# A decoder layer on one core: values kept at 64 features a head, and heads joined by the output matrix afterwards

## What is computed

```python
xn = layernorm(x) * gamma
q = (xn @ w_q).reshape(b, n, 16, 64); k, v = split(xn @ w_kv)
q = l2norm(q) * q_scale; k = l2norm(k) * k_scale
sim = einsum('bhid,bhjd->bhij', q, k) * 8 + dist * slope, causally masked
out = einsum('bhij,bhjd->bhid', softmax(sim), v)
x1 = layernorm(x + out.reshape(b, n, 1024) @ w_out)
x2 = layernorm(x1 + cross_attention(x1, ctx)); x3 = layernorm(x2 + ffn(x2))
```

## Time and profile before

| | |
|---|---|
| median of 3 runs (lowest to highest) | 1008.93 us (1008.55 to 1009.18) |
| the profiled execution | 1014.34 us, span 1012.2 us |
| mean granted clock of TensorE | 0.969 of full |
| PE busy | 849.9 us, 84% |
| DVE busy | 802.7 us, 79% |
| ACT busy | 660.7 us, 65% |
| POOL busy | 425.7 us, 42% |

### The profile page before, as it was taken

The page is one execution under the profiler, slowest core; times in us unless marked ns, Lnnn a source line. Parts: engine busy times, 40 slices in busy tenths (PEclk is TensorE's granted clock), DMA queues, the critical chain, the costliest instruction groups (busy, mean ns, idle before and its releaser), DMA issues.

```text
span 1012.2 us, 18717 instructions
## 1 busy us (share of the span) xinstructions
PE 849.9 (84%) x6181; PEld 663.4 (66%) x6181; DVE 802.7 (79%) x2564; ACT 660.7 (65%) x1938; POOL 425.7 (42%) x356
## 2 busy tenths in 40 slices
PE   6898888888888898888889889888888888888774
PEld 5667666765766676576767657666765766676552
DVE  6665779788888978898897888788787988888545
ACT  4475767757685766767676675767667576766532
POOL 0244162543616253361635346173534617253431
PEclk9799999999999999999999999999999999999795
DMA  6000000000100000000100001000100001000000
GB/s 189 6 1 6 6 27 7 6 12 6 28 12 6 6 13 26 6 6 12 27 6 7 11 6 28 11 6 7 27 11 7 6 12 27 1 6 6 6 1 10
DMA packets 26414, 15.56 MB, mean 15 GB/s; under 512 B 4304, under 2 KB 25552, under 8 KB 26320
## 3 DMA queue, kind: packets, MB, share of 16 engines
q1 hardware_dynamic: 26320, 14.38, 5.0%
HBM read 12.27 MB, written 2.10 MB: 14 GB/s over the span
## 4 chain that ended last, share of the span: by engine, by line
PE 45%; DVE 25%; ACT 18%; issue 6%; POOL 4%; DMA 2%; DVEq 0%; ACTq 0%; POOLq 0%
PE psY L600 12%; ACT pr L1319 9%; PE psS L566 6%; PE psT L586 5%; PE psS L636 4%; ACT sq L1291 3%; POOL pr L1519 3%; PE psJ L441 3%; PE psS L548 3%; PE psJ L443 2%; PE psJ L442 2%; DVE xp L1061 2%; DVE xmax L1059 2%; DVE ssq L957 2%; ACT xpT L1367 2%
## 5 line engine op out<-in xcount | busy, mean ns | idle before, releaser
L1519 POOL TENSOR_TENSOR pr<-pr,rden 128x512 f32<-128x512 f32 x192 | 192.9, 1040 | 379.2 <-ACT pr L1319 195.8
L600 PE MATMUL psY<-val,pT 128*128 128x128 f32 x1536 | 206.5, 281 | 31.3 <-ACT pT L1334 23.7
L1319 ACT ACTIVATE pr<-pr,nmin 128x256 f32<-128x256 f32 (+1 forms) x512 | 225.3, 443 | 10.8 <-DVE nmin L1004 10.2
L600 PEld LDWEIGHTS psY<-val,pT 128*128 128x128 f32 x1536 | 186.6, 193 | 41.8 <-issue 22.2
L1004 DVE CUSTOM_DVE_ANT_0 pr<-psS,alibi,nullmin 128x256 f32<-128x256 f32 (+1 forms) x512 | 183.7, 414 | 26.4 <-PE psS L566 24.4
L1510 POOL TENSOR_TENSOR qk<-qk,rn 128x1024 f32<-128x1024 f32 x64 | 121.1, 1913 | 88.8 <-DVE x L870 50.2
L586 PE MATMUL psT<-ident,pr 128*128 128x128 f32 x768 | 116.9, 279 | 20.2 <-POOL pr L1519 20.2
L566 PE MATMUL psS<-kT,qT 64*128 64x256 f32 (+1 forms) x1024 | 111.7, 346 | 19.3 <-DVE nmin L1004 12.9
L586 PEld LDWEIGHTS psT<-ident,pr 128*128 128x128 f32 x768 | 88.9, 143 | 39.9 <-POOL pr L1519 32.7
L566 PEld LDWEIGHTS psS<-kT,qT 64*128 64x128 f32 x1024 | 78.2, 189 | 48.5 <-DVE nmin L1004 19.4
L1319 ACT ACTIVATION_READ_ACCUMULATOR pr<-pr,nmin 128x1 f32 x512 | 96.6, 189 | 0.0
(11 more groups left out here) (138 smaller groups left out, 1663.5 us busy)
## 6 DMA issues: line engine op xcount, KB each, us to landing
w1s<-w1b SPq DMA_DIRECT2D x8, 258.0 KB, 2.9
xin<-x SPq DMA_DIRECT2D x16, 128.0 KB, 2.1
xres<-x SPq DMA_DIRECT2D x16, 128.0 KB, 2.1
w2s<-w2T SPq DMA_DIRECT2D x8, 256.0 KB, 3.2
out<-x SPq DMA_DIRECT2D x16, 128.0 KB, 1.8
pr<-w_q SPq DMA_DIRECT2D x1, 512.0 KB, 3.8
pr<-w_kv SPq DMA_DIRECT2D x1, 512.0 KB, 5.0
pr<-wvT SPq DMA_DIRECT2D x1, 512.0 KB, 4.5
```

Source lines behind the costliest of these rows:

```text
L600: mm = pe.matmul(psY[t], pT[c % 4][:, P * j:P * (j + 1)], val[:, kt, P * h:P * (h + 1)], start=(blk == 0), stop=False)
L1319: act.activation(pr[t][:, h, :], pr[t][:, h, :], ACT.Exp, bias=nmin[:, t, h:h + 1], scale=-1.0, accum_out=dparts[:, t, h, 0:1]).then_inc(e ...
L1519: pool.tensor_tensor(pr[t][:, hs, :], pr[t][:, hs, :], rden[:, t, hs].unsqueeze(2).broadcast_to([P, heads, P * (t + 1)]), ALU.mult).then_i ...
```

## The change

The two matrices are no longer merged. Values stay at 64 features a head: `project_v` has four chunks, `val` is half as wide. `weigh_values` swaps the operands: the value block (64 columns) is the stationary side and the turned probabilities (128 columns) move, and the result is the head's output, features on the partitions, in the lower or upper 64 partitions by the parity of the head. Heads of a pair are written next to each other. Four pairs fill a bank (psY for tile 0, S2 and S0 for tile 1), ACT copies it to `aoT`, and `join_heads` multiplies it by the output matrix: four products of 128 x 128 for each half of the heads of a tile, into `psY[t]`. There are four `copy_aoT` and sixteen joining products a sequence. `copy_qk(.., 0)` goes from DVE to ACT and the one `copy_v` of DVE is dropped. `xn_turn` and `split_xnT` move to the very start of an iteration. In the tail, one `turn_qk` pair goes ahead of `cross_q` and `merge_cross_heads`, and all four V chunks lie there.

```diff
-V_CHUNKS = 8
-QK_DVE, QK_ACT = (0, 1, 3), (2, 4, 5, 6, 7)
-V_DVE, V_ACT = (2,), (0, 1, 3, 4, 5, 6, 7)
+V_CHUNKS = 4
+QK_DVE, QK_ACT = (1, 3), (0, 2, 4, 5, 6, 7)
...
             def weigh_values(b, c):
...
-                    mm = pe.matmul(psY[t], pT[c % 4][:, P * j:P * (j + 1)], val[:, kt, P * h:P * (h + 1)],
-                                   start=(blk == 0), stop=False)
+                    pair, r = h // 2 - 4 * g, slice(DH * (h % 2), DH * (h % 2) + DH)
+                    mm = pe.matmul(bank[r, P * pair:P * (pair + 1)], val[:, kt, DH * h:DH * (h + 1)],
+                                   pT[c % 4][:, P * j:P * (j + 1)], start=(kt == 0), stop=(kt == t))
                 mm.then_inc(pv_done, 1)
+
+            def join_heads(b, t, g):
+
+                pe.wait_ge(aoT_copied, AC * b + 2 * t + g + 1)
+                if g == 0:
+                    take('Y', y_added, NT * b + t + 1)
+                for k in range(4):
+                    pe.matmul(psY[t], aoT[g][:, P * k:P * (k + 1)], wo[:, 4 * g + k, :],
+                              start=(g == 0 and k == 0), stop=False)
...
+                join_heads(i, 0, 0)
+                join_heads(i, 0, 1)
+                weigh_nulls(i, 0)
+                if a:
                     project_qk(i + 1, 6)
...
+            def copy_aoT(b, t, g):
+                act.wait_ge(pv_done, PC * b + (TILE_PC[0] if t else 0) + (TILE_PC[t] // 2) * (g + 1))
+                bank = psY_bank if t == 0 else psS[2] if g == 0 else psS[0]
+                act.activation(aoT[g][:], bank[:], ACT.Copy).then_inc(aoT_copied, 1)
```

More of the change, by code:

```diff
@@ L66 @@
 XC = 4
+AC = 4
 def slopes():
@@ L177, in program @@
         kT = sb("kT", [P, HP, SEQ])
-        val = sb("val", [P, NT, H * P])
+        val = sb("val", [P, NT, HD])
+        aoT = [sb(f"aoT{k}", [P, 512]) for k in range(2)]
         xres = sb("xres", [P, NT, P])
@@ L221, in program @@
         wqk_raw = pr[1][:, 0:8, :].rearrange("p h k -> p (h k)")
-        wvT_s, wout_s = (pr[1][:, 8 + 4 * k:12 + 4 * k, :].rearrange("p h k -> p (h k)")
-                         .rearrange("p (c d) -> p c d", c=HP) for k in range(2))
+        wv_raw = pr[1][:, 8:12, :].rearrange("p h k -> p (h k)")
         wqT_s = pr[0][:, 0:8, :]
@@ L587, in turn_probs, with group_bank @@
                 mm.then_inc(probsT_ready, 1)
+            def group_bank(t, g):
+                return psY_bank if t == 0 else psS[2] if g == 0 else psS[0]
             def weigh_values(b, c):
                 t, first = (0, 0) if c < TILE_PC[0] else (1, TILE_PC[0])
+                group = TILE_PC[t] // 2
+                g, within = divmod(c - first, group)
                 if c == 0:
[L592 to L595 removed]
+                    pe.wait_ge(v_copied, V_CHUNKS * (b + 1))
+                if within == 0:
+                    take('Y' if t == 0 else 'S2' if g == 0 else 'S0', aoT_copied, AC * b + 2 * t + g + 1)
                 evacuated(b, c)
[L597 removed]
+                bank = group_bank(t, g)
+                blocks = [0, 1, 2, 3] if t == 0 else [0, 2, 1, 3]
+                for j in blocks:
                     blk = 4 * (c - first) + j
                     h, kt = blk // (t + 1), blk % (t + 1)
[L600 to L601 removed]
+                    pair, r = h // 2 - 4 * g, slice(DH * (h % 2), DH * (h % 2) + DH)
+                    mm = pe.matmul(bank[r, P * pair:P * (pair + 1)], val[:, kt, DH * h:DH * (h + 1)],
+                                   pT[c % 4][:, P * j:P * (j + 1)], start=(kt == 0), stop=(kt == t))
                 mm.then_inc(pv_done, 1)
+            def join_heads(b, t, g):
[5 more added lines that the diff above has]
+                              start=(g == 0 and k == 0), stop=False)
             def turn_nulls(b, t):
@@ L782, in iteration @@
                         turn_nulls(i, 1)
-                weigh_nulls(i, 1)
+                join_heads(i, 1, 0)
                 if c:
-                    pe.wait_ge(y_added, NT * i + 1)
                     turn_cross_probs(i - 1, 0)
                     turn_cross_probs(i - 1, 1)
-                for k in range(4):
-                    if a and k < 3:
-                        project_v(i + 1, k)
-                    if k == 2:
-                        cross_q(i)
-                    if c and k == 0:
-                        weigh_cross_values(i - 1, 0)
-                        turn_cross_probs(i - 1, 2)
-                        turn_cross_probs(i - 1, 3)
-                    if c and k == 1:
-                        weigh_cross_values(i - 1, 1)
-                    if k == 1:
-                        x1_turn(i)
-                    if c and k == 3:
-                        merge_cross_heads(i - 1)
+                join_heads(i, 1, 1)
+                weigh_nulls(i, 1)
+                if a:
+                    project_v(i + 1, 0)
+                if c:
+                    weigh_cross_values(i - 1, 0)
+                    turn_cross_probs(i - 1, 2)
+                    turn_cross_probs(i - 1, 3)
+                if a:
+                    project_v(i + 1, 1)
+                if c:
+                    weigh_cross_values(i - 1, 1)
+                if a:
+                    project_v(i + 1, 2)
+                x1_turn(i)
                 for k in range(4):
@@ L806, in iteration @@
                         turn_qk(i + 1, 2 * k + 1)
-                    if a and k < 3:
-                        project_v(i + 1, 3 + k)
+                    if k == 0:
+                        cross_q(i)
+                        if c:
+                            merge_cross_heads(i - 1)
+                        if a:
+                            project_v(i + 1, 3)
                     if a and c and k == 2:
```

121 lines of the change are left out of this document (45 added, 76 removed).

## The result

The changed kernel takes 1032.5 us (median; 1030.3 to 1042.7) against 1008.7 before in the same session: a ratio of 1.025, 95% interval 1.019 to 1.031. The forecast was 1016 with a range of 996 to 1030, so the direction was right and the loss, +24 instead of +7, larger than the range allowed.

The account below looks back on a forecast made before the run. No single engine bounds it: ACT is last in the head, PE nearly the limit in the middle, DVE last in the tail. +12 over 14 iterations and the ends gave +7 on the profiled 1014.3, 1021; for the median 1016, range 996 to 1030.

Parts of the forecast that it names:

- Head, -2.3: First mask to POOL's norming of tile 0, ACT last: 7.95 us instead of 10.26, a gain of 2.3 an iteration.
- Middle, +0.2: Norming to second cross scores: gains spent on the joins, 15.0 us against 14.77, so +0.2 an iteration.
- rival 4: ACT's evictions bind: two more a sequence, 1.19 us, all on the path; 1028 us, chance 0.05.
- TensorE's sum, -102 us: TensorE alone: products 6.9 and V chunks 3.2 less, joins 3.7 more; 6.4 us less a sequence, times 16.
- Tail, +3.0: Second cross scores to next first mask: late null products +1.15, cross heads +0.35, third norm's seed +0.6, split +0.92.
- my walk: Tail steps from V's third chunk (567.75) to cross heads (570.5) and `add_y2` at 570.55 against 569.03: +1.5 in all.
- Sum, +0.9 an iteration: Head, middle and tail together, -2.3 + 0.2 + 3.0, in the 14 iterations with all three sequences: +12 us.
- rival 3, the clock: TensorE idles some 0.8 us twice in the tail, bringing the lower clock in most iterations: 1023 to 1030, chance 0.15.
- the ends: Outside those 14 iterations: about -3.5 us in iteration 15, -1.5 at the start and iteration 0.
- Rival 1: The tail absorbs the joins, its two extra delays under 0.6 us in sum: -0.6 an iteration, 995 us, chance 0.23.
- Rival 2: Product pairs do not overlap, a 64-column product costs 0.124 us: +1.8 an iteration, 1041 us, chance 0.07.

Follow-up runs that it names:

- the experiment on the head: Head put back in the old order, in the changed kernel with cross heads first and the filler ahead of tile 1's products kept: 1033.2 us, ratio 1.023.
- the repeated run: The changed kernel timed once more, as it is, against the kernel before: 1032.6 us, ratio 1.0225.

## Why the prediction was right or wrong

**Head, -2.3.** Right: 8.03 against 10.26 is -2.23, and the norming starts 8.03 us after the mask where I had 7.95; the null exponentials start at 7.03, where I had 7.05. With the old order of the head put back, only 0.8 of the 2.23 is left although the value projections are gone: 1.44 of the gain is bought by the split's early place, whose 0.92 I had booked under the tail.

**Middle, +0.2.** Right: +0.04 to +0.06, and the second cross scores wait for nothing. A block of eight products saves the 0.30 us that I had: 0.59 from start to start (669.86 to 670.45) against 0.89. The third block waits for `aoT` as forecast, 0.57 us (below, at rival 4).

**TensorE's sum, -102 us.** Wrong, though it carried no term of the forecast. The page shows -16, and one even iteration at full clock 48.23 us of busy TensorE against 49.96: -1.7, not -6.4. The step was "96 x (0.134 - 0.062)". 0.134 was a group's busy time over its count, and the rows of pipelined matmuls overlap their successors: a block of eight is busy for 1.06 us, but the next row starts 0.89 later (553.96 to 554.85), 0.111 each. Counted up to the next row's start (or their own end, where a wait follows), the products of an iteration take 11.4 us before and 6.8 after (0.119 and 0.071 each). So 4.6 is saved, 3.2 more with the V chunks, and the joins take 3.9 back. Another 1.2 goes to the turns of probabilities, for which I had no change, and the remaining 1.0 to rows that now stand behind waits, most of it the turns of q and k.

The new product is 0.59 / 8 = 0.074 in blocks of eight and 1.03 / 16 = 0.064 in the tail's sixteen; I had 0.062. Two blocks of eight are 1.18, one of sixteen 1.03: some 0.15 us comes with each block. The old product shows no such cost (0.89 for eight, 1.94 to 1.98 for sixteen). The four turns between two blocks pay about as much once more, 0.58 (670.45 to 671.03) against 0.44 before (553.52 to 553.96); where rows of another kind follow them, they take 0.41 in the changed kernel too (687.03 to 687.44). Before:

```profile
553.52 0.60 PE L586 MATMUL psT<-ident,pr 128*128 128x128 f32 x4
553.96 1.06 PE L600 MATMUL psY<-val,pT 128*128 128x128 f32 x8
554.85 0.60 PE L586 MATMUL psT<-ident,pr 128*128 128x128 f32 x4
```

and after, behind the two rows of 669.86 and 670.45 shown above:

```profile
671.03 0.66 PE L596 MATMUL psY<-pT,val 128*64 128x128 f32 x8
```

The Trainium skill (TensorEngine Tiling (Array Packing), Key Properties) says that a change of tiling mode drains TensorE. It gives no size. The trace agrees in that both the products and the turns cost about 0.15 us more where they alternate; no run isolates the change itself.

**Tail, +3.0.** The direction and the three waits were right, the size slightly low: +3.44 in this even iteration, +3.53 in an odd one. By its terms, from second cross scores on:

| step | before | after | measured | forecast |
|---|---|---|---|---|
| `add_y(1)` | 17.61 | 18.77 | +1.16 | +1.15 |
| `add_y2`, beyond that | 7.92 | 8.92 | +1.00 | +0.35 |
| third norm's step, beyond that | 2.53 | 3.26 | +0.73 | +0.6 |
| next first mask, beyond that | 5.32 | 5.87 | +0.55 | +0.92 |

The mis-sized term is the second: I let the cross heads come at +1.5 in all, they came at +2.16. In my walk the key eviction started as soon as `x1T` was out and the heads followed `xoT` at once. In the trace the third chunk ends 0.24 later than in the walk, ACT waits 0.22 for the turned keys, and the heads are there 0.81 after their start, and not 0.55 as in the walk. Three delays of a quarter of a microsecond along one chain make up what is missing. The last term was too high by 0.37: with the cross heads late in the kernel before, this step is 5.11, so the split costs 0.76 (as in the experiment on the head), and the late third norm gives 0.21 back. The first term came out to the hundredth but is not what the tail hangs on: taking 0.88 of it away made the iteration longer, because the chain through the cross heads ends later than DVE's.

**Sum, +0.9 an iteration.** It is +1.25 even and +1.36 odd: 18 us instead of 12.

**What I left at 0.15: rival 3, the clock.** This is the step that failed: the sum has nothing for the clock. I had named it, but in the tail, from waits for `qT` and x2, and against it I put the mean clock of the kernel before, which says nothing of a kernel that waits elsewhere. In iterations 1 to 14 no stretch begins behind the waits for `qT` and x2. They begin behind the head's waits (1.1 to 1.2 and 1.4 us, where 0.57 and 1.19 stood before), behind the wait ahead of tile 1's products (1.34, as before) and, once, behind the one ahead of the last sixteen (1.40; 1.08 before). This last place, 37.3 to 38.7 us after a first mask, has one such stretch in seven of the profiles, with the fillers as without.

Shown: filling three waits raises the clock (between 0.954 and 0.970 without, between 0.974 and 0.976 with them) and takes about 7 us off, at an unchanged undisturbed iteration, and does the same with the cross heads first (1013.3 to 1007.4). Filling the head's alone moved neither clock nor time. Which stretches a filler removes shows only over all profiles, in iterations 1 to 14. Stretches that begin 4.1 to 4.5 us after a first mask: 13 in the seven profiles of this head order without a filler there (three of them have none), none in the four with one. Stretches that begin 28.4 to 29.4 us after it: 11 in the eight profiles of this change without a filler ahead of tile 1's products (two have none), none in the four with one. Not shown: why the changed kernel falls to the lower clock behind a wait that the kernel before has too, and what the middle filler does alone, since I never ran it without the others in this order.

**The account.** 18 us of longer iterations and 7.6 of clock; the repeated run lost 23.3, so -2.6 is left for the ends, where I had -5 (the last iteration is 80.4 to 81.3 us in the two profiles after, 82.6 before). Against the forecast that is 6 us from the tail's sum, 7.6 from the clock and 2.4 from the ends. The direction came out right because the tail's arithmetic was nearly right, the number left the range because all of them added to the same side.

**The other rivals.** Rival 1: the two extra delays of the tail are 1.73 in sum, far above its 0.6. Rival 2: refuted by the products' rows and by their other order. Rival 4: ACT waits 1.75 us for the last products before it copies `aoT` in the tail, so the eviction is not late there. In the middle one is: TensorE waits 0.57 us for it before the third block, which my middle had counted (+0.2, measured +0.04).

```profile
673.91 1.14 PE L596 MATMUL psY<-pT,val 128*64 128x128 f32 x16 [0.57 <-ACT aoT L1300]
...
696.22 0.60 ACT L1300 ACTIVATE aoT<-psS 128x512 f32<-128x512 f32 x1 [1.75 <-PE psS L596]
```

The Trainium skill (TensorEngine Tiling (Array Packing), PSUM Bottleneck) warns that evictions may bind once TensorE is faster. The trace shows one such wait, these 0.57 us, of the four copies of a sequence; what ACT cost beyond it came from the order of its queue (12 us).

**What the change is worth.** The late cross heads, with ScalarE's order there, cost the kernel before 30 us. With them first and the waits covered, the changed kernel is 0.2% faster than before; what its new products, joins and head gain together is small, and the reordering in the same edit takes many times as much.

## What to carry to other kernels

When an edit both changes work and reorders it, price the order by itself first: move only the two lines in the old kernel and look at the same waits. Take the price of pipelined matmuls from start to start, never from busy time over count. And when work is taken out of places where it covered a wait of TensorE, look for half-clock stretches there, in more than one profile, since they come and go from one execution to the next; a filler is a quick test of whether they cost anything.

## What the runs showed of the hardware that was not expected

- A 64-column product costs 0.074 us in blocks of eight and 0.064 in the tail's sixteen, and four turns between two such blocks cost 0.58 us instead of 0.44. The order of halves is worth at most 0.003 us an instruction: 1.08 against 1.03 for sixteen.
- Unread products in three waits of 1.1 to 1.4 us made the kernel about 7 us (0.7%) faster. Two kernels with one undisturbed iteration (59.66) differ by this much, and beside the fillers the runs show no difference between them but the granted clock (0.954 to 0.970 and 0.974 to 0.976).
- A wait of 1.34 us ahead of tile 1's products stands in both kernels. The kernel before has no half-clock stretch behind it in iterations 1 to 14, with the cross heads early or late; the changed one has 11 in the eight profiles without a filler there.
- A stretch there costs 2.8 to 3.2 us in an odd iteration and 1.4 to 1.5 in an even one, one in the head 1.0 to 1.5.
